# State-space layer: the four step sizes of a chunk move by one unit, and three counters become one

## What is computed

```python
xz = hidden_states @ in_proj_w.T
x, z = jnp.split(xz, 2, axis=-1)                  # 512 channels each
x = silu(causal_conv(x, conv_w) + conv_b)         # 4 taps along time
A = -jnp.exp(A_log)                               # 512 x 16
dt, Bm, C = jnp.split(x @ x_proj_w.T, [16, 32], axis=-1)
dt = jax.nn.softplus(dt @ dt_proj_w.T + dt_proj_b)
def step(h, ins):
    dt_t, B_t, C_t, x_t = ins
    dA = jnp.exp(dt_t[:, :, None] * A)
    h = dA * h + dt_t[:, :, None] * B_t[:, None, :] * x_t[:, :, None]
    return (h, jnp.einsum('bdn,bn->bd', h, C_t))
y = scan(step) + x * D
return y * silu(z) @ out_proj_w.T
```

## Time and profile before

| | |
|---|---|
| median of three runs | 3368.63 us (3365.46 to 3370.95) |
| the profiled execution | 3368.68 us, of which the span from the first to the last instruction is 3367.0 |
| busy share of the span | PE 86%, DVE 65%, ACT 42%, POOL 36% |
| mean granted TensorE clock | 0.909 of full speed |
| the chain that ended last | PE 50%, DVE 26%, issue 10%, ACT 5% |
| the loop of the last stage | from 2301.85 us, the start of unit 0 of chunk 0 |

### The profile page before, as it was taken

The page is one execution under the profiler, slowest core; times in us unless marked ns, Lnnn a source line. Parts: engine busy times, 40 slices in busy tenths (PEclk is TensorE's granted clock), DMA queues, the critical chain, the costliest instruction groups (busy, mean ns, idle before and its releaser), DMA issues.

```text
span 3367.0 us, 45234 instructions
## 1 busy us (share of the span) xinstructions
PE 2878.9 (86%) x14054; PEld 1313.5 (39%) x14055; DVE 2203.8 (65%) x3070; ACT 1425.5 (42%) x2463; POOL 1199.6 (36%) x1360
## 2 busy tenths in 40 slices
PE   6994698888988988869999997878788888989876
PEld 5662133232332332236666665752222222222212
DVE  3576866766766767022222222646999999999997
ACT  2341065665655655712222221425445445545442
POOL 1143021221112212210000001825777767777675
PEclk9996598998988989979999998998898999998978
DMA  6166413133132130041111112620000000000000
GB/s 200 63 215 145 138 41 46 26 63 53 27 57 44 42 47 23 18 131 31 31 31 31 31 31 80 210 96 7 3 17 13 7 13 20 7 13 13 13 1 19
DMA packets 175061, 176.60 MB, mean 52 GB/s; under 512 B 50674, under 2 KB 151541, under 8 KB 174749
## 3 DMA queue, kind: packets, MB, share of 16 engines
q1 hardware_dynamic: 168732, 157.52, 18.7%
q0 software_dynamic: 6144, 16.82, 1.5%
HBM read 100.46 MB, written 73.83 MB: 52 GB/s over the span
## 4 chain that ended last, share of the span: by engine, by line
PE 50%; DVE 26%; issue 10%; ACT 5%; DMA 2%; POOL 2%; SPq 1%; another core or an unknown queue 1%; POOLq 0%; DVEq 0%; ACTq 0%; PEldq 0%
PE ps L1668 47%; DVE hh L1634 10%; DVE mp L1405 6%; DVE ps L1621 3%; POOL Ch L890 2%; PE ps L1876 2%; DMA ks<-qk_parts 1%; ACT Pt L1013 1%; DVE dt L1608 1%; DVE tl L1607 1%; DVE q L1317 1%; SPq L528 1%; PE ps L1832 1%; SPq L619 0%
## 5 line engine op out<-in xcount | busy, mean ns | idle before, releaser
L1405 DVE TENSOR_REDUCE mp<-ps 128x1 f32<-128x1024 f32 (+7 forms) x768 | 669.5, 909 | 276.0 <-PE ps L1668 245.7
L1013 ACT ACTIVATE Pt<-ps 128x512 f32<-128x512 f32 (+3 forms) x1280 | 611.6, 539 | 519.0 <-PE ps L1668 487.6
L890 POOL TENSOR_TENSOR Ch<-hh,Cb 128x1024 f32<-128x1024 f32 x256 | 603.7, 2358 | 72.6 <-DVE hh L1634 72.6
L1668 PE MATMUL ps<-ks,qs 96*128 96x512 bf16 (+3 forms) x1280 | 395.8, 382 | 117.8 <-DVE mp L1405 68.5
L1634 DVE TENSOR_TENSOR_SCAN hh<-dA,hst,ps 128x512 f32<-128x512 f32 x384 | 473.1, 1263 | 0.0
L766 POOL TENSOR_SCALAR_AFFINE_SELECT Pt<-Pt 128x128 f32<-128x128 f32 x512 | 147.8, 294 | 880.0 <-ACT Pt L1013 870.6
L1668 PE MATMUL ps<-dtx,pick 32*128 32x512 f32 x1024 | 326.0, 697 | 139.9 <-DVE hh L1634 139.1
L1668 PE MATMUL ps<-qs,ks 99*128 99x512 bf16 (+3 forms) x1280 | 413.3, 370 | 18.6 <-ACT Pt L1013 15.9
L1193 ACT ACTIVATE dA<-ps 128x1024 f32<-128x1024 f32 x256 | 261.8, 1023 | 392.4 <-PE ps L1668 392.1
L1621 DVE TENSOR_TENSOR ps<-ps,Bb 128x512 f32<-128x512 f32 x512 | 325.4, 680 | 32.9 <-PE ps L1668 32.4
L1668 PE MATMUL ps<-dt,WA 32*128 32x512 f32 x1024 | 322.0, 707 | 20.3 <-ACT dA L1193 20.1
(11 more groups left out here) (303 smaller groups left out, 3765.2 us busy)
## 6 DMA issues: line engine op xcount, KB each, us to landing
W<-in_L_ffn_w SPq DMA_DIRECT2D x16, 1024.0 KB, 12.0
qk_parts<-q SPq DMA_DIRECT2D x32, 384.0 KB, 2.9
qs<-qk_parts SPq DMA_DIRECT2D x96, 128.0 KB, 6.2
ks<-qk_parts SPq DMA_DIRECT2D x96, 128.0 KB, 8.7
expert_out<-yb SPq DMA_DIRECT2D x72, 128.5 KB, 2.5
expert_in<-zero SPq DMA_DIRECT2D x9, 1024.0 KB, 11.4
xg<-expert_in SPq DMA_DIRECT2D x72, 128.0 KB, 2.7
X<-in_L_attn_x SPq DMA_DIRECT2D x4, 1024.0 KB, 9.5
```

The source lines that it names most:

```text
L890: pool.tensor_tensor(Ch[:, k % 6, :, :], hh[:, k % HRING, :, :], Cb[:, par:par + 1, :].broadcast_to([P, 2, CH]), ALU.mult).then_inc(s_Ch, 1)
L1013: act.activation(Pt[:, n % PRING, q0:CH], ps[:, 4 + n % SRING, q0:CH], ACT.Exp, scale=SCALE).then_inc(s_exp, 1)
L1405: dve.tensor_reduce(mp[:, qc, h, t % TPC, k0 // 1024:k0 // 1024 + 1], slot[:, 0:n], AX.X, ALU.max).then_inc(s_free, 1)
L1668: return pe.matmul(o, lhsT, rhs, start=start, stop=stop, **kw)
```

## The change

Of the seven step sizes of chunks 1 to 7 of each block, block 0 moves from unit 28 to 29 and blocks 1, 2, 3 from units 0, 4, 8 to 1, 5, 9. In chunk 0 blocks 2 and 3 move from units 9 and 13 to 12 and 14. Nothing is moved on the other engines. In the first stage the counters `s_nrm_abs`, `s_nrm_ps` and `s_sc` (the absolute values are there; the norms are in PSUM; the scale is there) become one, `s_nrm`, which the three events raise in turn to 1, 2 and 3; ScalarE waits once, for 3, in place of twice.

```diff
-        s_nrm_abs, s_nrm_ps, s_sc, s_scaled = sem("s_nrm_abs"), sem("s_nrm_ps"), sem("s_sc"), sem("s_scaled")
+        s_nrm, s_scaled = sem("s_nrm"), sem("s_scaled")
...
-            act.activation(gb[:, :, :, :], ga[:, :, :, :], ACT.Abs).then_inc(s_nrm_abs, 1)
-
-            act.wait_ge(s_sc, 1)
-            act.wait_ge(s_nrm_ps, 1)
+            act.activation(gb[:, :, :, :], ga[:, :, :, :], ACT.Abs).then_inc(s_nrm, 1)
+
+            act.wait_ge(s_nrm, 3)
...
-            dve.wait_ge(s_nrm_ps, 1)
+            dve.wait_ge(s_nrm, 2)
...
-                if n == 0 and u in (5, 9, 13):
-                    step_size(0, u // 4)
-                if n + 1 < NC and u == 28:
+                if n == 0 and u in (5, 12, 14):
+                    step_size(0, {5: 1, 12: 2, 14: 3}[u])
+                if n + 1 < NC and u == 29:
                     step_size(n + 1, 0)
-                if n and u in (0, 4, 8):
+                if n and u in (1, 5, 9):
                     step_size(n, u // 4 + 1)
...
-            pe.wait_ge(s_nrm_abs, 1)
+            pe.wait_ge(s_nrm, 1)
...
-            last.then_inc(s_nrm_ps, 1)
+            last.then_inc(s_nrm, 1)
```

## The result

| | median, us | runs | range |
|---|---|---|---|
| before | 3369.22 | 20 | 3364.52 to 3372.28 |
| changed | 3362.18 | 20 | 3357.18 to 3366.34 |

What follows compares the result with a forecast made beforehand. VectorE was taken to bound the scan. Terms 2.7 (21 steps) + 3.0 (mask waits) + 1.1 + 2.3 (chunk 0) and 0 for the counters give 9.1 us: 3368.6 - 9.1 = 3359.5 us, range 3351 to 3368.5.

Steps and rivals of the forecast that it cites:

- The bound: In the last stage's scan VectorE sets the time, busy 1013 of 1056 us; its instruction costs reach the end nearly one for one.
- The series avoided, the delayed Ch met: In units 29, 1 and 5, 21 steps avoid GpSimd's series but meet its pushed-back big product Ch: 1.30 us loss becomes 1.17.
- The rule from the earlier trace: A step-size instruction on VectorE loses about its overlap with a GpSimd tensor product, less 0.09 us, whichever product it is.
- The size of it: Moving 21 steps to units 29, 1 and 5 saves 21 x (1.30 - 1.17) = 2.7 us; extremes 23 and -3.2.
- Chunks without a saved state: Shorter units, GpSimd further behind: if the overlap with Ch reaches 1.45 us, the 21 moved steps save -3.2 us.
- The mask waits: VectorE's four waits for ScalarE's mask ahead of unit 28's step go, as the step comes a unit later: 3.0 us.
- nobody new waits for it: TensorE's spread for the new chunk's first unit, issued behind unit 29, still follows the moved step; no new wait, 0 us.
- TensorE hands part of it back: Rival: TensorE idles at steps, its clock falls, costing VectorE 0.5 to 1 us a chunk, 3.5 to 7 us; 26 in 100.
- Chunk 0: Unit 9's step moved to 12 saves 1.1 us; unit 13's moved to 14 is paid from idle near unit 18, 2.3 us.
- The 1.1 of the step of unit 12: In chunk 0 the step moved from unit 9 meets only Ch's tail, not a series: 1.30 - 0.2 = 1.1 us saved.
- Free odd slots: Rival: moved steps in odd units lose only 0.2 us each, saving 23.1, with other terms 29.5 us, 3339 us; 6 in 100.
- The slower case, over the SiLU of z: Rival: clock falls behind steps of units 29 and 1 delay ScalarE's first decay; 3370 to 3381 us, say 3376; 6 in 100.

Runs made afterwards that it cites:

- the short series: Changed kernel with GpSimd's series of chunks 2 to 7 on 1 column in place of 512: 3306.51 us, ratio 0.9949 to the kernel before.
- the series apart: Changed kernel with GpSimd's series moved so that neither of the two units ahead of a step size was to have one: 3352.72 us, ratio 0.994.
- The run with block 0 alone: Kernel before with only block 0's step size moved from unit 28 to 29: 3373.13 us, ratio 0.9996.
- the three other traces with this order: Kernel before with only chunk 0's steps moved (3370.26 us), the run with block 3 in unit 14 (3295.26 us) and the short series (3306.51 us).
- the run with block 3 in unit 14: Changed kernel with block 3's step size of chunks 1 to 7 moved from unit 9 to 14: 3295.26 us, ratio 0.9912 to the kernel before.

## Why the prediction was right, and where it wasn't

**The bound.** Right. VectorE sets the loop, and its busy time and waits account for all but 0.6 us of the change.

**The series avoided, the delayed Ch met.** Right. With 18 of the 21 copies freed from it, in the short series, the loop is 11.7 us shorter still. The two odd slots of the earlier trace rows in which no step size stood foretold what the copy would meet; the copies read 1.55 to 2.00 us in 19 of 21 places, 16 of them within the forecast 1.7 to 2.0, and the other two instructions are at 0.69 everywhere but in unit 5 of chunk 0. The short series shows it directly. The rule from the earlier trace rows, the overlap less 0.09 us, gave 1.17 for 1.26; the copy of chunk 6 shown above lost 1.14. All 31 copies in the changed kernel's loop start beside a Ch, and all lose the overlap less 0.09 to 0.12 us, for overlaps from 0.14 to 1.42 us; with the series apart one of 2.12 us cost 1.99. So a copy that starts while a GpSimd product runs hardly gets on until that ends, whichever product it is. By the Trainium skill's rule (SBUF — State Buffer, "Who interferes with whom": the first to start keeps the shared ports to its end) the loss would be the full 1.26, and the trace agrees to 0.12.

The rule was too narrow in one point. It named GpSimd's tensor products alone, but the series' TENSOR_SCALAR costs too. The kernel before, GpSimd beside the step of the earlier trace rows:

```profile
2960.15 0.95 POOL L861 TENSOR_SCALAR dtx<-te 128x512 f32<-128x512 f32 x1
```

The addition that starts at 2960.70, 0.40 us ahead of its end, takes 0.95 in place of 0.69, and in all fourteen steps of units 0 and 4 it is 0.94 or 0.95. And where VectorE started first it is GpSimd that takes longer: this TENSOR_SCALAR takes 0.62 alone, and the series product of 1.57 in the earlier trace rows takes 1.27. The sum didn't suffer, since the present loss was taken from the busy times.

**The size of it.** Too small: 2.7 us forecast, 6.1 in the trace; the busy sum of the three lines fell to 91.6, where about 94 was forecast. The new loss was taken from one chunk, 1.17; it is 1.02 in the mean of the 21. Chunks without a saved state, where the prediction feared 1.45, have overlaps of 0.97 to 1.12, and in two places (unit 5 of chunks 3 and 5) VectorE waited for TensorE in unit 4, 0.50 and 0.83 us, GpSimd caught up meanwhile, and the copy took 0.98 and 0.91. So a part of what looks like a gain there was paid by a wait elsewhere: of the 6.1 us 3.8 lie in unit 5, against 1.5 us of new waits in unit 4.

**The mask waits.** The term came in as forecast, 3.0 us, but the step "nobody new waits for it" failed. The run with block 0 alone shows 3.9 us leaving VectorE and 4.3 coming back as waits for TensorE.

**TensorE hands part of it back.** This rival had 26 in 100 and 3.5 to 7 us. It happened beside the forecast, not in place of it: 5.0 us in the loop. The place was only partly the one named: unit 4 has 1.5 us of waits in three chunks (and 0.7 in unit 8 are gone); 3.7 lie near unit 18, behind an idle stretch that is there before and after, where the clock was lower than before in chunks 1 and 2 and higher in chunk 5. I had set "VectorE waits for it at nearly one place a chunk only" against this rival; it was the very place. The prediction took those waits as fixed.

**Chunk 0.** The idle stretch did pay for the step: 2.5 us for 2.3. That the two are so near is luck: in the three other traces with this order the wait shrinks by 3.6 us and 0.8 to 1.0 more is waited in unit 26. The 1.1 of the step of unit 12 came to 0.7, since the series of unit 10 had Ch still late there (0.81 us of overlap, copy 1.41 us).

**The other two.** Free odd slots: fell, by the copies. The slower case, over the SiLU of z: no wait for ScalarE's decay shows in the changed kernel, and unit 4's waits stayed below 0.9 us.

**The sum** was 9.1 for a measured 7.0 (4.4 to 9.1): its two large errors, 3.4 us in the steps and 5.0 in TensorE's waits, have opposite signs and largely cancel. That the sum came out near is in part luck; the terms say more than it does.

## What to carry to other kernels

Moving VectorE's two-input work away from a GpSimd burst isn't enough: count how late GpSimd then is with its regular work, product by product, and place the work where it has caught up. Here GpSimd lost 1.0 us with each series and regained 1.1 in a unit without one; with one series and two free units behind it, all copies of unit 1 were at 0.73 to 0.94. Look first at what idle stretch is left, for work of the bounding engine that can be moved under it costs nothing; here that was worth 20 us of the loop, over twice what the change under study brought there. And a wait whose length holds a slower TensorE clock is no constant: two orders of the same instructions gave 1.8 and 5.0 us for it.

## What the runs showed of the hardware

A COPY_PREDICATED of 128 x 512 that starts beside a running GpSimd product loses their overlap less 0.09 to 0.12 us, in all 31 copies of the changed kernel's loop. The scans show none: those with a saved state take 1.27 us in the median, beside a Ch (203 of them in the changed kernel) as beside no product (46).

There are 3.2 us between two identical stretches of TensorE's work, at 2.4 GHz the one and partly at 1.2 GHz the other, behind the same 2.53 us of idle. In chunks 1 to 6 VectorE's waits behind such stretches came back to 0.01 us in a second trace of the changed kernel, while the stages ahead of the loop took 39 us less there. Yet the order of the work alone does not settle it: in chunk 0, behind the same 1.84 us of idle, with the same order of work in the loop so far, the clock fell in the two traces of the changed kernel and stayed up in the run with block 3 in unit 14. What decides between the two stays open. Pauses of 1.66 us and less kept the clock at 1.00 in chunk 1 of that run, but in its chunk 2 it fell behind such a pause.
